# A new merge of twelve streams of steps in a four-layer transformer kernel on one Trainium2 core

## The reference, cut to what matters

```python
# layer 0: windowed attention, 16 heads of 64, 4 key/value heads, window 64
q, k = rmsnorm(x @ wq.T), rmsnorm(x @ wk.T)
attn = softmax(where((i >= j) & (i - j < 64), q @ k.T / 8, -inf)) @ v
# layer 0: 8 experts of 128 -> 256 -> 128 with gelu, the best two per token
# layer 1: causal attention with rotary positions, 32 score maps; 8 experts
#          of 128 -> 352 -> 128, silu(gate) * up, the best two per token
# layer 2: attention, 16 heads of 8; a projection with a mixture of low-rank parts
# layer 3: linear attention; a feed-forward part with dequantized integer weights
```

## Time and profile before

| | us |
|---|---|
| median of three runs | 1311.14 |
| lowest and highest | 1306.95, 1311.45 |
| the profiled execution | 1302.39 |
| its span in the trace | 1300.6 |
| mean granted TensorE clock of it | 0.953 |

### The profile page before, as it was taken

The page is one execution under the profiler, slowest core; times in us unless marked ns, Lnnn a source line. Parts: engine busy times, 40 slices in busy tenths (PEclk is TensorE's granted clock), DMA queues, the critical chain, the costliest instruction groups (busy, mean ns, idle before and its releaser), DMA issues.

```text
span 1300.6 us, 23823 instructions
## 1 busy us (share of the span) xinstructions
PE 1183.6 (91%) x9238; PEld 699.4 (54%) x9238; DVE 900.8 (69%) x1863; ACT 695.3 (53%) x1678; POOL 339.0 (26%) x349
## 2 busy tenths in 40 slices
...
GB/s 235 61 1 1 58 48 124 113 131 50 39 36 18 98 4 33 131 143 70 133 104 93 111 140 188 108 62 27 104 3 99 102 26 76 3 2 31 1 9 25
DMA packets 71468, 92.41 MB, mean 71 GB/s; under 512 B 9846, under 2 KB 55670, under 8 KB 69766
## 3 DMA queue, kind: packets, MB, share of 16 engines
...
## 4 chain that ended last, share of the span: by engine, by line
PE 74%; DVE 12%; POOL 5%; ACT 4%; issue 3%; DMA 2%; SPq 0%; DVEq 0%; ACTq 0%
PE psB L428 37%; PE psA L428 30%; PE psB L432 5%; POOL slots_x L1934 2%; DVE mx L1462 2%; POOL tH L1947 2%; PE psA L432 2%; ACT pbuf L1795 1%; DMA wA<-slots_x 1%; DVE st L1170 1%; DVE pbuf L1183 1%; DVE arena L1090 1%; ACT pbuf L1709 1%; DVE st L1173 0%; DVE pbuf L1191 0%
## 5 line engine op out<-in xcount | busy, mean ns | idle before, releaser
L1795 ACT ACTIVATE pbuf<-psA 128x512 f32<-128x512 f32 (+3 forms) x768 | 351.1, 489 | 218.0 <-PE psA L428 211.4
L1462 DVE TENSOR_REDUCE mx<-psA 128x1 f32<-128x512 f32 (+3 forms) x520 | 326.1, 660 | 76.8 <-PE psA L428 74.0
L428 PE MATMUL psA<-arena 64*64 64x128 f32 (+6 forms) x1504 | 152.8, 292 | 3.9 <-DVE mx L1462 1.6
L1709 ACT ACTIVATE pbuf<-psA,st,rq 128x128 f32<-128x128 f32 x256 | 113.5, 459 | 66.4 <-DVE st L1173 66.0
L428 PE MATMUL psB<-pbuf,arena 128*64 128x128 f32 (+4 forms) x1536 | 130.7, 388 | 12.8 <-ACT pbuf L1721 12.2
L428 PEld LDWEIGHTS psA<-arena 64*64 64x64 f32 (+3 forms) x1504 | 83.7, 137 | 62.6 <-ACT pbuf L1795 33.3
L428 PE MATMUL psA<-arena,w 96*128 96x512 bf16 (+4 forms) x320 | 112.7, 410 | 1.3 <-ACT pbuf L1721 1.0
L428 PE MATMUL psA<-w_mdiagT,w_identb 128*128 128x128 bf16 x512 | 108.8, 220 | 0.0
L1851 POOL CAST arena<-tF 16x512 bf16<-16x512 f32 (+2 forms) x24 | 14.5, 605 | 318.2 <-DVE tF L1471 245.8
L428 PE MATMUL psB<-xf,wA 128*128 128x128 f32 x624 | 93.2, 294 | 0.3 <-DVE xf L1328 0.3
L428 PEld LDWEIGHTS psB<-xf,wA 128*128 128x128 f32 x624 | 81.9, 204 | 6.4 <-issue 2.0
...
## 6 DMA issues: line engine op xcount, KB each, us to landing
...
```

Of the source, the lines that this page charges most:

```text
L428: return pe.matmul(out, lhsT, rhs, start=start, stop=stop, skip_group_check=True)
L1462: dv.tensor_reduce(m[:, t, h:h + c], maxb(lay, b, n)("mx", lay, b, n)[:, 0:c * k].rearrange("p (c k) -> p c k", c=c), AX.X, ALU.max) \
L1709: a = ac.activation(sm[:, k, :], S[:, P * k:P * k + P], ACT.Exp, bias=st[:, 4 + k:5 + k], scale=rq(b)[:, 4 * h + k, kv, x:x + 1], accum_ou ...
L1795: ac.activation(pb(lay, b, s, j)[:, 0:T - q0_], scoreb("ex", lay, b, s, j)[:, 0:T - q0_], ACT.Exp, bias=0.0, scale=1.0) \
```

## The change

Only the string `MERGE` is replaced. The streams, the steps, their operands and their waits are the same, and each stream keeps its own order; what changes is how the twelve are interleaved.

```diff
--- before.py
+++ after.py
@@ -25,31 +25,31 @@
 MERGE = (
-    "12aca2lcl2c2lcl2c2l3clcl2c2lcl2clcl4cl2cl3cl2clclc2lcb3cb2cjb2cjcbjbcjbj2cj2c2j2c5j2cbc3jcb2cb3cbcjc"
-    "2jcjcb2cl3jcj3cj2cb2c2j3cjlj2cjcljlb2lj2lbj2lj3l3jc2bl2cl2c2j2lcjljl5j3ljb2j3bj2cj2cj8cjbljb3j6c2jc2"
...
+    "12a2ca2lcl2c2lc2lcl3cl2clclclcl3clcl4cl3cl2clcl2c3l2cb3cbj2cbc3jbcb3cjcb2jc2jbcjb2j3cjc2jbjcj2cbjcj2"
+    "cjcjcj3c2j6cb2cljcj2c2jlj3cbljljljb3lblclj2ljlblcj2ljcjlcbjcl2jl2jljljcj2clcjbcj2c2b3cj2c2j4cbc2j2cl"
...
```

More of the change, by code:

```diff
@@ new lines @@
+    "cjcjcj3c2j6cb2cljcj2c2jlj3cbljljljb3lblclj2ljlblcj2ljcjlcbjcl2jl2jljljcj2clcjbcj2c2b3cj2c2j4cbc2j2cl"
+    "jl3cjcb2jl2jl5c2jb2cjcbcjc2jb4jb2jcl3cb2cjb2c2jc2j2cjcb4cj3c2jc2jbj2c2j4c2bj2c2jcjcjbcj5cjcjcj2c3l2j"
+    "4lc2l2cljlc2l5cj2lc2lbjcjbcbcbjcjcj4cjljlj3c3jcl2jblbjbjl2jbj3ljlcjljlajlbjabl2jab2jb2jljljljlbjbjl2"
+    "jbjlcjb4jl2jl2jljcja2jb2jbc2j2dj2bjc2jdjb2djajbjb2jdjajb2jd2jb2jbja3jbjdjbjc2j2b2jeje2jbejajej2eje3j"
+    "ebj2e2j3e2jejeaj2ej2ejcej2ea3ea3ea3ecec2e2c7ed7ec4edec2eb2ed2becebdkbebdb2e4bebekbk2bdbe2bkebe3bdkbk"
@@ new lines @@
+    "cb3e2bkbebec2bebkc2bebkebebkebcb2eckbebce2bdkebcbeck2b2ebc2b2e2bedebkeckebcebd2b2eke2bdek2ebcbec2bce"
+    "bekbebcbekebebkb2ebcbecbcecek2bk2bebebdbk2bebk2bcecebdcbkbebkdbecbe2cbebkebek2be2bke2b2ecbebcbkcebkd"
+    "bebed2bk2bebecbkebebcbekcbebebkbecbebkbcek2b2ebcbebek2bcekbekcbkbecebdebebkebebkek2bc2beck2b2eck2beb"
+    "ebeckbdc2bekcebc2bckbcbcb2cebkcbecbebke2cbebcebekbebebecbke2bkbek2e2bcebc2bceb2cbe2ckec2bekb2cb2e2be"
+    "bkbkbcece2b2cek2ebc2bck2bd2bekebcbk2bd2ebck2b2e3b2kcbebe2cbe2bekbebk2ebce2cbebce2bk2ce2bkcbecbcbcebk"
@@ new lines @@
+    "cebecbcecekbebebebekec2bekebcbecebeb2ceckcecbcbcbkbc2e4cbe2b2ebkb2ecebkbecekbebece2be2bdebkebek2bc2e"
+    "c2beb2c2eckbeckcke2cbcbcebec2bekeckececkdebc2bcebckbecebk2b2ek2bekbebecece2bcedce2bcececdeckebcbkcbe"
+    "bcbebebcb2c2ec2ke2bkebecbce2bebebekbebebkcebekb2ececbece2cbececbecbekbcebcececbebceb2e2ce2cebcb2kb2e"
+    "cecbkbcecbcebcbcec2b2k2ecbecece2cebebe3bek2ebebkbebk2bebkbe3bebkbeb2ebebk2bke2b2e2bk2bkebe2bebe2bek2"
+    "bkebkbkbcebab2ebebek2bebk2bcbebek2b2ek4bce2bekbeke4bk2bcakbkbae2bkcd2ke2bd2bcbkbe2bdek3bkcbekbebaebk"
@@ new lines @@
+    "2bc2bk3bdbe2bkbkabdebebebk2bekebe3bkbe2bebkbe2beb2ebkebebkbebke2bk2be2bekebabebek2bkebed2bk2bedebek2"
+    "bedbe3bke2bebkb2ebk2be2bke3bebk3bebk2bebkb2ebkbcebebk2bkbebe2bebk2bebk2e2ba2bk2ekcbe2bebke2bebe2beb2"
+    "kebek2bkabebebkb2ebkekebdebebakbe2ba2b2ekebekebebebebkb2ebk2bedaebkebebaebde2bkb2e2bedebebdke2b2ek2b"
+    "ek2e2b2e2bkebebkbedb2e2bkb2ebebkebebkbebebedb2ebkbebedbebec2e2kebedke2bebeke2bekb2ebkebebkbebebebebk"
+    "beb2ekb2ebkb2ebkbebebebebebekb2ebebebebkebebkebebe2bekbekebebebebk2b2ebkbe2bebkbebekbekbebeb2ebe2bek"
```

7 lines of the change are left out of this document (4 added, 3 removed).

## The result

| | before | changed |
|---|---|---|
| median of four runs, us | 1309.05 | 1360.56 |
| lowest and highest | 1304.57, 1311.45 | 1357.33, 1367.48 |
| the profiled execution's span | 1300.6 | 1365.6 |
| its mean granted clock | 0.953 | 0.936 |

What follows compares the result with a forecast made beforehand. PE, 91% busy, was taken as the bound, with other engines or chains setting the pace ahead of 562 us. Terms summed to +10.3 us on 1302.4, 1313; 8.8 us for the median made 1321 us, range 1303 to 1337.

Steps and rivals of the forecast that it cites:

- (a): First expert layer, groups 1 to 5: exponentials on ACT ahead of the copy of st lengthen the turns, +8.9 us.
- (b): First tokens: work done ahead of 199 us moves behind it, group 2's tokens come at 217.5 us, +3.9 us.
- (c): POOL's ks0 of batch 1 comes 10 us later behind eight more scatters, covered by PE's wait for tokens: 0.
- (e): Up to 150 us: VectorE sets the pace, reordering moves idle time either way: 0, bounds -4 and +4 us.
- (d): First expert layer, groups 6 to 9: group 8's parted gelu costs +2 us, a shrinking 4.25 us wait gives -2.5.
- (f): 455 to 492 us: eleven more reductions mx ahead of the second sorting, in VectorE's idle time: -2 us.
- (g): Second scatter: the last one comes 6 to 9 us later, net cost 0, bounds -1 and +7 us.
- (h): Behind 562 us: PE is full, rows of ex, pv and mx shift one or two places: 0, bounds -2 and +3.
- Rival 3: Slower, chance 0.20: longer turns lower PE's granted clock from 199 to 350 us to 0.84; +22 us, 1333 us.
- Rival 1: Faster, chance 0.17: PE's in-order stalls set the first expert layer; -10 us, 1301 us.
- rival 2: No change, chance 0.21: the first expert layer runs late but layer 0's attention sets 350 to 455 us; within 6 us, 1313.

Runs made afterwards that it cites:

- p1_st: Before's order with, in groups 1 to 5 of the first expert layer, the exponential steps sc ahead of the copy st: 1.0164 of before, +20 us.
- k1_head_b: Second run of the changed order up to the tokens of group 0, then the order of before: 0.9950 of before, -9 us.
- e1_ks0: Changed order with xt of batch 0's third quarter moved behind ks0 of batch 1, as in before: 1.0412 of before.
- e4_wl: Changed order with step stack of batch 2 moved behind weight load wl of block 7 in the second expert layer: 1.0133 of before, 1434.3 us.
- r3_ring_wl: Before's order to the end of the first expert layer, then the changed one with block 7's weight load ahead of stack: 1.0176 of before.
- r2_before_ring: Before's order to the end of the first expert layer, then the changed order: 1.0126 of before, 1433.5 against 1414.8 us.
- k1 to k4: Changed order up to group 0's tokens, first expert layer's end, layer 1's batch 2 exponentials, or layer 3's fg3, then before's: 0.9985, 1.0086, 1.0166, 1.0200.
- the second measurement: The changed kernel itself measured again beside before on another chip: 1.0376 of before, profiled span 1348.0 us.
- after_third: The changed kernel a third time, on a chip where before is slower: 1.0267 of before, 1453.4 against 1416.6 us.

## Why the prediction was wrong

By its own steps, each with what the table has for it:

- **(a) ACT in groups 1 to 5, +8.9.** The mechanism was right for the copy, the term was sized too small: +12.6 between 150 and 190 us of PE's work, and +17.6 with nothing else changed (p1_st: 74.7 us there, against 57.1 in k1_head_b, which has before's ring). The copy stood 7 us behind the gelu, as worked out (6.6). What failed is the step from there to a turn: turns grew from 12.5 to some 15 us as forecast, but the turn with group 4's parted gelu went from 11.5 to 20.3 us, which is +8.7 and not +3.1. There the second half waits for a table load, a step and a load, and PE, in order, waits with it for 3.87 us. The forecast's "less the room that PE left there" had no row behind it. One sign didn't come either: the tokens of groups 3 to 6 were to find PE idle 3 to 5 us each for their DMA, and it was 0.81, nothing, 1.94 and nothing. PE had other work between them and waited for ACT's gelu and for `tp` instead; in p1_st, which has the late copy alone, the waits for the DMA did come in three turns of five.
- **(b) first tokens, +3.9**, and **(c) `ks0`, 0.** Together +6.6 (13.1 lost, 6.5 caught up), inside (b)'s bounds. (c)'s cover holds, as e1_ks0 shows, and the place of the loss is as told: what was done ahead of the tokens is left over. One premise failed: the last scatter did not start "at 193.86 as before" but at 196.89, since the burst began 2.6 us late, about what (e) had lost, and the tokens landed 3.3 us later. Group 2's tokens stood at 221.8, not 217.5; 3.3 us of the 4.3 are that, the turn itself took 19.6 us where 18.6 was forecast.
- **(d) -0.5, (f) -2, (e) 0.** (d) and (f) lie in the 190 to 345 us of work, which cost +1.9 where -2.5 was forecast; (e) cost +3.1, within its bounds.
- **(g) 0.** +4.8, within the bounds of -1 and +7. The rows for the mechanism were right, the value in the middle of them was a hope.
- **(h) everything behind 562 us, 0, bounds -2 and +3: the step that failed most.** It cost 19 us (2.2 + 6.0 + 6.3 + 4.7 - 0.2). The reason given was "PE is full". That is the reason why nothing can be *won* there, and it was read as if nothing could be lost: a wait that an order newly makes on a full PE is lost at its place in full, and little behind it catches up (taking one out gave back all 6 us in e4_wl's profile, some 2 of 6 in r3_ring_wl's). That the order behind the first expert layer costs time by itself is shown by r2_before_ring (+19 us on its chip). The prediction showed no row of SP's queue for that part; the queue's difference is five exchanges in the whole program, and one of them is the 6 us. The other 13 us have no such cause shown.

From the forecast's 10.3 to the table's 48.0 us it is 37.7: (h) 19.0, (g) 4.8, (d) with (f) 4.4, (a) 3.7, (e) 3.1, (b) 2.7. Rival 3, the clock, named the wrong stretch: from 199 to 350 us the clock was 0.90 before, and it is 0.94 in the counterpart from 218 to 378. The clock did cost, but in the last stretch, by 14 to 18 us in some executions and none in others. Rival 1 fell with the result, whose copy in group 2 stands 7 us behind the gelu where it needed 4, and rival 2 with k1 to k4. The first result's four runs hold one such execution at least, so part of its size is chance; the second measurement's 50 us, with a profiled execution without it, show that the loss doesn't rest on that. The table load takes 1.28 us (240.66) and the next exponential starts 0.01 us behind its end, as before; so the drain of which the Trainium skill tells ("ScalarE: Activation LUTs", section "What ACT_TABLE_LOAD costs") isn't seen here either, and its 8.3 us are no part of what was missed.

What stays open: the small losses from 470 to 950 us of work (11 us, of which PE's idle time is 5.7) have no single place, and it stays open why e4_wl takes 19 us less than after_third on another chip of the same kind, when the exchange explains 6 us and the last stretch 8 (before differs by 2 between the two chips); in the two profiled executions 5 us more lie ahead of 132 us of PE's work, where the orders are the same. What the head of the order costs on a chip of the first kind was read from traces alone.
